# Softmax-free attention denominators: one product for four tiles and a spreading product, in place of a small product, a widening copy and two transposes per tile

## The reference

```python
qkv = (x @ qkv_w.T + qkv_b).reshape(b, l, 3, NUM_HEADS, HEAD_DIM)      # 16 heads of 16
q = jax.nn.relu(q) + FEATURE_EPS
k = jax.nn.relu(k) + FEATURE_EPS
kv = jnp.cumsum(jnp.einsum('bhld,bhle->bhlde', k, v), axis=2)
k_cum = jnp.cumsum(k, axis=2)
num = jnp.einsum('bhld,bhlde->bhle', q, kv)
den = jnp.maximum(jnp.einsum('bhld,bhld->bhl', q, k_cum)[..., None], DEN_EPS)
out = num / den
```

## Time and profile before

| | |
|---|---|
| time, median of 3 runs | 453.91 us (452.8 to 456.64) |
| time of the profiled execution | 452.43 us |
| span of the profiled execution, first to last instruction | 450.6 us |
| PE busy | 401.9 us, 89% |
| DVE busy | 297.7 us, 66% |
| POOL busy | 257.0 us, 57% |
| ACT busy | 187.9 us, 42% |

### The profile page before, as it was taken

How to read it: one execution, slowest core, us unless ns; L and a number is a source line. 1 busy time by engine, 2 the same in 40 slices (tenths; PEclk the granted TensorE clock), 3 DMA queues, 4 the chain that set the end, 5 groups by cost and what they waited for, 6 DMA issues and landing times. The chain is left out here.

```text
span 450.6 us, 11500 instructions
## 1 busy us (share of the span) xinstructions
PE 401.9 (89%) x3890; PEld 285.9 (63%) x3890; DVE 297.7 (66%) x981; ACT 187.9 (42%) x460; POOL 257.0 (57%) x382
## 2 busy tenths in 40 slices
PE   7988999999999999999999999998995696968860
PEld 2555667777777677767776777776663464556640
DVE  3635777777877887778587678655552876726851
ACT  3253454454554454455355345443652342123210
POOL 5135665567566646764657575776677646403326
PEclk9999999999999999999999999998998799789985
DMA  8970670000000000000000000000002112511124
GB/s 241 336 218 1 204 225 13 14 13 23 16 13 14 26 15 13 14 25 14 15 14 25 14 14 13 25 15 25 25 15 91 47 47 95 176 48 47 57 74 140
DMA packets 27026, 27.71 MB, mean 61 GB/s; under 512 B 3499, under 2 KB 25912, under 8 KB 26968
## 3 DMA queue, kind: packets, MB, share of 16 engines
q1 hardware_dynamic: 24440, 22.22, 15.6%
q0 software_dynamic: 1120, 3.36, 2.6%
q10 hardware_dynamic: 1408, 1.39, 0.9%
HBM read 14.64 MB, written 12.32 MB: 60 GB/s over the span
## 5 line engine op out<-in xcount | busy, mean ns | idle before, releaser
L1486 POOL TENSOR_TENSOR s_t<-s_t,causal 128x512 f32<-128x512 f32 x64 | 80.1, 1272 | 20.2 <-ACT s_t L827 20.2
L447 PE MATMUL bank<-h1t,w_qkv 128*128 128x512 f32 x112 | 55.3, 617 | 1.0 <-DVE x L1077 0.8
L1491 POOL TENSOR_SCALAR ve<-mv 128x3 f32<-128x3 f32 x36 | 7.1, 197 | 82.4 <-DVE mv L1124 82.1
L1095 DVE TENSOR_TENSOR s_t<-sbank,causal 128x512 f32<-128x512 f32 x64 | 40.8, 678 | 0.3 <-PE sbank L468 0.3
L1149 DVE TENSOR_TENSOR attn_t<-bank,rden_t 128x256 f32<-128x256 f32 x32 | 13.6, 425 | 40.8 <-PE bank L563 35.1
L827 ACT ACTIVATE rden_t<-bank 128x256 f32<-128x256 f32 x32 | 12.3, 383 | 66.9 <-PE bank L435 66.9
L680 PE MATMUL sbank<-h1t,w 128*128 128x512 f32 x72 | 37.8, 666 | 0.5 <-ACT h1t L827 0.5
L454 PE MATMUL bank<-w_qkv,h1t 128*128 128x256 f32 x128 | 36.0, 404 | 1.4 <-DVE arena L1033 1.1
L496 PE MATMUL bank<-s_t,vp 128*32 128x128 f32 x1024 | 35.4, 280 | 1.8 <-POOL s_t L1486 1.8
L468 PE MATMUL sbank<-arena 32*128 32x256 f32 x512 | 36.9, 402 | 0.0
L827 ACT ACTIVATE s_t<-sbank 128x512 f32<-128x512 f32 x64 | 34.4, 593 | 0.0
(11 more groups left out here) (217 smaller groups left out, 926.2 us busy)
## 6 DMA issues: line engine op xcount, KB each, us to landing
rows<-x SPq DMA_DIRECT2D x32, 128.0 KB, 1.7
out<-x SPq DMA_DIRECT2D x8, 512.0 KB, 2.9
x<-in_x SPq DMA_DIRECT2D x7, 512.0 KB, 7.4
we<-in_we SPq DMA_DIRECT2D x1, 2048.0 KB
rows<-zeros SPq DMA_DIRECT2D x1, 1408.0 KB, 7.8
xmask<-in_mask POOLq DMA_DIRECT2D x2, 616.0 KB, 7.4
we<-in_we SPq DMA_DIRECT2D x1, 1024.0 KB
arena<-rows SPq DMA_DIRECT2D x2, 512.0 KB, 5.5
```

The source lines that it names most:

```text
L447: mm = pe.matmul(dst[:, :], w_qkv[:, ch, cb * P:(cb + 1) * P], h1t[:, g % 3, ch, :], start=(ch == 0), stop=(ch == CH - 1))
L1095: dve.tensor_tensor(s_t[:, r, :, :], sbank[r][:, :].rearrange("p (s q) -> p s q", s=4), causal[:, :].unsqueeze(1).to_broadcast([P, 4, P]), ...
L1486: pool.tensor_tensor(s_t[:, r, :, :], s_t[:, r, :, :], causal[:, :].unsqueeze(1).to_broadcast([P, 4, P]), ALU.mult)\
```

## The change

The denominators of a whole group are computed at once, at the top of the steps with i % 4 = 0. Eight products (two halves for each of four tiles) have a 32-column table `to_heads` as the stationary side and the 128 tokens of a tile as the moving side; the four tiles go to four bands of 32 partitions. The result is 128 x 128: heads on partitions, tokens along the row. VectorE takes maximum and reciprocal once per group, over 128 x 128. For each tile two products (`spread`, 32 rows by 128 columns as the stationary side, from a second table `to_feats`) repeat each head's reciprocal to its 16 features; they stand at the top of the next step. The copy `rdx` and its two transposes go. `to_feats` is the transpose of `to_heads`, made once before the loop.

Three things change their place. On TensorE the cross scores of tile B now stand ahead of the values of tile V. On VectorE the scans and multiplications of the running key sum, and the group's maximum and reciprocal, now stand between the cross maximum and the multiplication to `attn_t`. On ScalarE the copy to `rden_t` moves behind the copy of h2.

The diff, cut to its core:

```diff
@@ -469,6 +471,28 @@
+            def denominators(g):
+                wait(pe, qkc_ready, 2 * g + 2)
+                wait(pe, den_ready, g)
+                wait(pe, rdt_ready, GT * g - 1)
+                for ch in range(CH):
+                    for j in range(GT):
+                        mm = pe.matmul(bank[2][32 * j:32 * j + 32, D:D + P], to_heads[:, ch, 0:32],
+                                       qkc(g % 2, ch)[:, tok(j)], start=(ch == 0), stop=(ch == CH - 1),
+                                       skip_group_check=True)
+                mm.then_inc(den_done, 1)
+
+            def spread(t):
+                wait(pe, rden_ready, t // GT + 1)
+                wait(pe, rdt_ready, t)
+                rows = slice(32 * (t % GT), 32 * (t % GT) + 32)
+                for ch in range(CH):
+                    mm = pe.matmul(bank[2][:, ch * P:(ch + 1) * P], to_feats[rows, ch, :], rden[rows, :],
+                                   start=(ch == 0), stop=(ch == CH - 1), skip_group_check=True)
+                mm.then_inc(rdt_done, 1)
@@ -507,12 +531,18 @@
                     mm.then_inc(t2_done, 1)
+                if is_tile(K) and K % GT == 0:
+                    denominators(K // GT)
+                if is_tile(M):
+                    spread(M)
                 if g < NG:
...
+                if i == 0:
+                    pe.wait_ge(prep_act, 8)
                 if is_tile(K):
                     wait(pe, qk_ready, 4 * (K // GT) + 2)
@@ -520,22 +550,11 @@
-                if is_tile(K):
-                    wait(pe, qkc_ready, 2 * (K // GT) + 2)
-                    wait(pe, rdt_ready, K)
-                    for ch in range(CH):
-                        mm = pe.matmul(bank[2][:, ch * HC:(ch + 1) * HC], qkc((K // GT) % 2, ch)[:, tok(K)], head8[:, :],
-                                       start=(ch == 0), stop=(ch == CH - 1), skip_group_check=True)
-                    mm.then_inc(den_done, 1)
...
-                if is_tile(V):
-                    wait(pe, qk_ready, min(4 * NG, 4 * g + i % GT + 1))
-                    wait(pe, x1_ready, i - 1)
-                    values(V)
                 if is_tile(B):
                     if is_tile(K):
                         wait(pe, ktok_ready, K + 1)
@@ -545,6 +564,10 @@
                     mm.then_inc(sc_done, 1)
+                if is_tile(V):
+                    wait(pe, qk_ready, min(4 * NG, 4 * g + i % GT + 1))
+                    wait(pe, x1_ready, i - 1)
+                    values(V)
@@ -565,16 +588,9 @@
                 if is_tile(K):
                     scores(K)
-                if is_tile(K):
-                    wait(pe, rdx_ready, K + 1)
-                    wait(pe, den_ready, K + 1)
-                    for ch in range(CH):
-                        mm = transpose(bank[2][:, ch * P:(ch + 1) * P], rdx[:, ch * P:(ch + 1) * P])
-                    mm.then_inc(rdt_done, 1)
@@ -624,6 +640,10 @@
+                pe.wait_ge(init_dve, 5)
+                for ch in range(CH):
+                    mm = transpose(bank[1][:, ch * P:(ch + 1) * P], to_heads[:, ch, :])
+                mm.then_inc(tab_done, 1)
@@ -858,6 +877,10 @@
+                if is_tile(M):
+                    wait(act, rdt_done, M + 1)
+                    wait(act, attn_ready, M - 1)
+                    copy(rden_t[:, M % 2, :], bank[2][:, 0:D]).then_inc(rdt_ready, 1)
@@ -874,11 +897,6 @@
-                if is_tile(K):
-                    wait(act, rden_ready, K + 1)
-                    wait(act, rdt_done, K)
-                    copy(rdx[:, :].rearrange("p (h e) -> p h e", e=HD),
-                         rden[:, K % 2, :].unsqueeze(2).to_broadcast([P, NH, HD])).then_inc(rdx_ready, 1)
@@ -1097,14 +1113,6 @@
-                if is_tile(K):
-                    wait(dve, den_done, K + 1)
-                    wait(dve, rden_ready, K)
-                    dve.tensor_scalar(den[:, :], bank[2][:, 0:NH], EPS, None, ALU.max).then_inc(den_ready, 1)
-                if is_tile(K):
-                    wait(dve, den_ready, K + 1)
-                    wait(dve, rdx_ready, K - 1)
-                    dve.reciprocal(rden[:, K % 2, :], den[:, :]).then_inc(rden_ready, 1)
@@ -1140,6 +1148,21 @@
                         .then_inc(nmx_ready, 1)
+                if is_tile(K) and K % GT == 0:
+                    wait(dve, den_done, K // GT + 1)
+                    wait(dve, rdt_ready, K)
+                    wait(dve, rden_ready, K // GT)
+                    dve.tensor_scalar(den[:, :], bank[2][:, D:D + P], EPS, None, ALU.max).then_inc(den_ready, 1)
+                    dve.wait_ge(den_ready, K // GT + 1)
+                    dve.reciprocal(rden[:, :], den[:, :]).then_inc(rden_ready, 1)
+                if g < NG:
+                    if i % GT in (1, 2):
+                        sum_keys(g, i % GT - 1)
+                    if i % GT == 3:
+                        for ch in range(CH):
+                            by_queries(g, ch)
                 if is_tile(M):
                     wait(dve, num_done, M + 1)
@@ -1158,12 +1181,6 @@
-                if g < NG:
-                    if i % GT in (1, 2):
-                        sum_keys(g, i % GT - 1)
-                    if i % GT == 3:
-                        for ch in range(CH):
-                            by_queries(g, ch)
@@ -1422,8 +1439,12 @@
-            dve.tensor_copy(head8[:, :], own_wide[:, :].rearrange("p (h v) -> p h v", h=HC)[:, :, HD])\
-                .then_inc(init_dve, 1)
+            dve.memset(to_heads[:, :, :], 0.0).then_inc(init_dve, 1)
+            dve.wait_ge(init_dve, 3)
+            own = own_wide[:, :].rearrange("p (h v) -> p h v", h=HC)[:, :, HD].unsqueeze(1).to_broadcast([P, GT, HC])
+            for ch in range(CH):
+                rows_of = to_heads[:, ch, :].rearrange("p (j h) -> p j h", j=GT)[:, :, HC * ch:HC * (ch + 1)]
+                dve.tensor_copy(rows_of, own).then_inc(init_dve, 1)
```

More of the change, by code:

```diff
@@ L71, in decoder_block @@
         own_wide = sb("own_wide", [P, HC * HV])
-        head8 = sb("head8", [P, HC])
+        to_heads = sb("to_heads", [P, CH, P])
+        to_feats = sb("to_feats", [P, CH, P])
         parity = sb("parity", [P, 2])
@@ L141, in decoder_block @@
         state = sb("state", [P, 3, CH, 2, HD])
-        den = sb("den", [P, NH])
-        rden = sb("rden", [P, 2, NH])
-        rdx = sb("rdx", [P, D])
+        den = sb("den", [P, P])
+        rden = sb("rden", [P, P])
         rden_t = sb("rden_t", [P, 2, D])
@@ L269, in decoder_block @@
         (t1_done, qk_done, v_done, s_done, ktr_done, st_done, t2_done, sc_done, num_done, den_done, ptr_done,
-         rdt_done, out_done, px_done, prep_pe, t3_done, x1_done, x12_done, ztr_done, y_done) = (
+         rdt_done, out_done, px_done, prep_pe, tab_done, t3_done, x1_done, x12_done, ztr_done, y_done) = (
             sem(f"pe_{n}") for n in ("t1", "qk", "v", "s", "ktr", "st", "t2", "xscore", "num", "den", "ptr",
-                                     "rdt", "out", "px", "prep", "t3", "x1", "x12", "ztr", "y"))
-        (s_copied, h1_ready, h1t_ready, ktok_ready, qpar_ready, h2t_ready, exp_done, pt_ready, rdx_ready,
+                                     "rdt", "out", "px", "prep", "tab", "t3", "x1", "x12", "ztr", "y"))
+        (s_copied, h1_ready, h1t_ready, ktok_ready, qpar_ready, h2t_ready, exp_done, pt_ready,
          rdt_ready, prep_act, h3_ready, h3t_ready, hx_ready, th_ready) = (
-            sem(f"act_{n}") for n in ("s", "h1", "h1t", "ktok", "qpar", "h2t", "exp", "pt", "rdx", "rdt",
+            sem(f"act_{n}") for n in ("s", "h1", "h1t", "ktok", "qpar", "h2t", "exp", "pt", "rdt",
                                       "prep", "h3", "h3t", "hx", "th"))
@@ L567, in step @@
                 if i == 0:
-                    pe.wait_ge(prep_act, 7)
                     pe.wait_ge(prep_dve, 6)
@@ L789, in _ @@
             prep(pe)
-            pe.wait_ge(init_dve, 3)
             pe.wait_ge(w_attn_in, 16 * 2)
@@ L889, in step @@
                                    accum_out=psum_[:, B % 2:B % 2 + 1]).then_inc(exp_done, 1)
-                if is_tile(K):
-                    wait(act, rdt_done, K + 1)
-                    wait(act, attn_ready, K - 1)
-                    copy(rden_t[:, K % 2, :], bank[2][:, 0:D]).then_inc(rdt_ready, 1)
                 if is_tile(B):
@@ L916, in prep @@
                 copy(c_score[:, :], sbank[2][:, 0:NB * KX]).then_inc(prep_act, 1)
+                act.wait_ge(tab_done, 1)
+                copy(to_feats[:, :, :].rearrange("p c n -> p (c n)"), bank[1][:, 0:D]).then_inc(prep_act, 1)
             def norm_h3(n):
@@ L1051, in by_queries @@
                 wait(dve, ksum_ready, 2 * g + ch + 1)
-                wait(dve, den_done, GT * (g - 1))
+                wait(dve, den_done, g - 1)
                 dve.tensor_tensor(qkc(g % 2, ch), ksum(g % 2, ch), qall(g % 2, ch), ALU.mult).then_inc(qkc_ready, 1)
```

## The result

| | before | changed |
|---|---|---|
| time, median | 453.94 us | 466.53 us (464.83 to 469.0) |
| ratio to before | | 1.0273, 95% interval 1.0207 to 1.0339 |
| span of the profiled execution | 450.6 us | 465.3 us |
| one step, mean of steps 2 to 26 | 8.96 us | 9.48 us |

The last row is worked out from the starts of the key transposes of steps 2 and 27: (274.02 - 50.09) / 25 before, (289.72 - 52.61) / 25 after. These 25 steps hold 13.2 of the 14.7 us between the two spans. The forecast was 464 us.

What follows compares the result with a forecast made beforehand. TensorE leads, but VectorE was to hold the projection: a step of 7.27 + 1.31 + 0.22 + 0.45 + 0.11 = 9.36 us against 8.96. 452.43 + 10.0 (25 steps) + 1.3 (outside) = 463.7, stated as 464; range 456 to 473.

Steps and rivals of the forecast that it cites:

- Block to state part: TensorE from block to state part: 4.14 us, a gain of 0.15; cross scores start 0.86 after the key transposes.
- VectorE ahead of the projection: Work moved ahead of `attn_t` on VectorE puts the output projection at 7.27 us in the mean, against 7.45 before.
- The spread: Two new products on TensorE's path between h2 transposes and next block: 0.45 us taken, 0.36 to 0.57 as bounds.
- The group's products: Eight products per group on TensorE: 0.45 us, per step 0.11 (0.09 to 0.14).
- the hold of 0.25: The output projection waits 0.25 us for VectorE: 7.27 against TensorE's own 7.02.
- rival 3: VectorE is in time for the projection: step 9.11, or 9.00 with cheap spread and group; 455 to 457 us; chance 0.15.
- The sign that it gave for being wrong: Steps under 9.1 us would mean VectorE doesn't hold the projection, or the spread is far cheaper.
- Outside these steps: Step 0, the preparation and steps 28 to 31, which have no block: together +1.3 us.
- The range: Total time 456 to 473 us, leaving out rival 2 and the end of the high units.
- the high units: Upper bound: scan 1.76, multiplications and reciprocal each 0.45 longer, spread 0.57, group 0.14; step 9.84, total 476 us.
- Rival 1: GpSimd, held by the scan, is 0.2 us late with h2 in three of four steps: +4, 468 us; chance 0.18.
- Rival 2: TensorE's work is all that counts: -13, 439 us, or 445 with the spread at 0.45; chance 0.09.

## Why the prediction was right, and where not

**Block to state part: right.** 4.14 forecast, 4.19 measured; the cross scores 0.86 after the key transposes, as said. That the removed product was worth nothing was shown by leaving it out, and the order by itself gave its small gain, though half of that came at the block and not here.

**VectorE ahead of the projection: wrong.** The forecast held the projection at 7.27, 0.25 behind TensorE; it was at 7.14, with TensorE's own time. Three numbers did it. The scan was taken at 1.54, the median of the earlier trace rows; it took 1.23, because in its new place it comes first and GpSimd waits. In the trace of before, VectorE's scan of step 14 stands behind a large GpSimd row:

```profile
162.83 0.73 POOL L1505 TENSOR_TENSOR x<-x,b_out 128x256 f32<-128x256 f32 x1
...
162.96 1.67 DVE L1046 TENSOR_TENSOR_SCAN arena<-arena,zero 128x512 f32<-128x512 f32 x1
```

It began 0.13 after GpSimd's row and took 1.67; the long durations of the earlier trace rows came with the old place. One transpose costs 0.17 on the way to the projection, not 0.10, which is the pitch behind two others. And the forecast laid VectorE's rows end to end, while most start 0.03 to 0.1 ahead of the recorded end of the last (the scan's end is 169.81 + 1.23 = 171.04, and `attn_t` starts at 170.95), and `attn_t` takes 0.40 in step 14 and 0.36 in step 16, not 0.42. This is what counts in step 16, which has no scan: `attn_t` was done 7.00 after the block, where the forecast's terms give 7.30. With 0.06 for the release VectorE was ready at 6.82 in step 14, 6.90 in step 15 and 7.06 in step 16, for 7.32, 7.08 and 7.36 forecast, and TensorE came at 7.14, 7.01 and 7.14. The hold is real only in steps without a state part (0.23 to 0.3 us), in three of these 25.

**The spread: the mis-sized term.** 0.45 was taken, from products that fill all rows; 0.63 and 0.09 of later start were measured. The run over 128 rows took 0.44: the 0.45 was right for it, and the band of 32 is what costs the rest. The 0.10 more in the block behind the band is no part of the miss, since the block took its 1.82 before the change too. The upper end, 0.57 from the state part's 32 x 32 tiles, was the nearer row. A record in the band takes 0.63 / 4 = 0.158. The Trainium skill (TensorE: Matmul & The Clock Gate, The mechanism) says that a weight load overlaps running matmuls only if its row group differs. For the band the trace agrees: 0.158 per record against 0.11 at full height, and the block's weights behind it start only with its product (173.97, 173.98). Between full-height products it does not agree, since there the row groups are the same and the block's weights still start 0.11 ahead (171.39, 171.50). That unhidden loads are the reason for the price of the band was not tested.

**The group's products: 0.45 forecast, 0.57 measured.** These have weights of 128 rows and 32 columns, so the band of rows isn't the reason. What the reason is stays open.

The errors partly offset: 9.36 forecast for the step, 9.48 measured. That the time lies near the forecast is in part luck: without the hold of 0.25 the forecast's own terms give 9.11 and 455 to 457 (its rival 3), and what filled the place is the spread, 0.27 dearer than taken. The sign that it gave for being wrong, steps under 9.1, could not show this. For a usual step the forecast was 9.25 without the group's share (7.27 + 1.31 + 0.22 + 0.45); -0.13 at the projection and +0.27 for the spread make it 9.39, as measured. The group's products make six of the 25 steps 9.83 to 9.96 long, 0.12 in the mean where 0.11 was taken. The short step 2 (8.85) and the three without a state part (9.26 to 9.32) bring it down by 0.03. **Outside these steps** the forecast added 1.3. The trace has +2.5 before step 2 and -1.0 behind step 27. Of the first, most is not of the change: the four other kernels that have nothing new ahead of the loop reached the first key transposes at 37.10 to 37.95, before at 35.40, the changed one at 38.05. **The range:** the high units' 0.45 for the slowest scan against the shortest is 0.56 by the earlier trace rows (1.76 - 1.20), which would put their end at 477 and not 476.

**Rival 1** was right in its mechanism: GpSimd's small row was held for the whole scan. In usual steps h2 was not late, so its 4 us did not come; in the three without a state part TensorE waited 0.03 to 0.05 for it. With the scans behind `attn_t` it waited 0.38 in step 17. By the Trainium skill's rule (SBUF — State Buffer, Who interferes with whom) the operation that comes second is blocked until the first is done; the trace agrees, 1.12 for 0.20. **Rival 2** (TensorE's work alone) fell with the small product. **Rival 3** had the projection right and the spread too cheap.

## What to carry to other kernels

Before you remove an operation, look what ends the idle time behind it: one that stands ahead of a wait is free, and its removal only lengthens the wait. Time a replacement by a row with the same shape of weights, rows and columns of the array both, and not only by the count of moving columns. A change made of several parts should be timed in parts: here two of them gain 0.8% together, and the third loses over 3%.

## What was not expected of the hardware

- A pair of float32 products with 32 x 128 weights and 128 moving columns takes 0.63 us, with 128 x 128 weights 0.44; it also starts 0.09 later behind a full-height transpose, and the 512-column block behind it takes 0.10 longer (1.82 for 1.72, start to start).
- A GpSimd operation on three columns takes 1.12 to 1.19 instead of 0.20 us when a 128 x 512 scan with both inputs in SBUF has begun 0.09 ahead of it. The scan itself then takes 1.22 to 1.29; 0.13 behind the start of a GpSimd addition of 256 columns it took 1.67, and 0.27 ahead of that addition 1.38, while the addition took 1.63 instead of 0.73.
